# A fused attention and mixture-of-experts kernel: the start and the first score items of its projection stage rearranged

## The reference

```python
x = x + _L0_attn_a_ref(_layernorm(x), Wq, Wk, Wv, Wo)      # this layer's projection is what changes
x = x + _L0_ffn_ref(_layernorm(x), ...)
x = x + _L0_attn_b_ref(_layernorm(x), ...)
x = x + _L0_ffn_ref(_layernorm(x), ...)

def _L0_attn_a_ref(x, Wq, Wk, Wv, Wo):
    q = (x @ Wq.T).reshape(Bx, Tx, H, dk)
    k = (x @ Wk.T).reshape(Bx, Tx, H, dk)
    v = (x @ Wv.T).reshape(Bx, Tx, H, dk)
    scores = jnp.einsum('bthd,bshd->bhts', q, k) / math.sqrt(dk)
    scores = jnp.where(causal_mask, -jnp.inf, scores)
    attn = jax.nn.softmax(scores, axis=-1)
    ...
```

## Time and profile before

| | us |
|---|---|
| median of 3 runs | 1771.57 |
| lowest and highest of them | 1766.8, 1778.27 |
| the profiled execution, whole | 1780.99 |
| its span (first to last instruction in the profile) | 1779.3 |
| TensorE busy in the span | 1642.0 |
| VectorE busy in the span | 1278.2 |
| projection stage, up to the last item's matmuls | 131.5 |

### The profile page before, as it was taken

How to read it: one execution, slowest core, us unless ns; L and a number is a source line. 1 busy time by engine, 2 the same in 40 slices (tenths; PEclk the granted TensorE clock), 3 DMA queues, 4 the chain that set the end, 5 groups by cost and what they waited for, 6 DMA issues and landing times. The chain is left out here.

```text
span 1779.3 us, 35884 instructions
## 1 busy us (share of the span) xinstructions
PE 1642.0 (92%) x11140; PEld 1206.5 (68%) x11141; DVE 1278.2 (72%) x2670; ACT 1048.0 (59%) x1851; POOL 796.1 (45%) x773
## 2 busy tenths in 40 slices
PE   7889999999999794999999998699975999999998
PEld 3454444444443683999999998344544999999997
DVE  5678788888882667677777776358886777777776
ACT  3336677776777443666666664546654666666664
POOL 5431112112121122666666665225542566666664
PEclk9999999999999875999999999899975999999999
DMA  4655254453531752332232222301112222222222
GB/s 138 188 142 130 86 135 111 114 131 103 121 96 49 159 184 70 86 47 48 48 49 48 48 49 36 109 1 48 48 47 82 45 47 47 47 47 47 47 47 38
DMA packets 102667, 140.85 MB, mean 79 GB/s; under 512 B 18160, under 2 KB 86768, under 8 KB 99504
## 3 DMA queue, kind: packets, MB, share of 16 engines
q1 hardware_dynamic: 65638, 90.88, 19.5%
q0 software_dynamic: 31808, 37.32, 13.0%
q10 hardware_dynamic: 5130, 11.54, 1.9%
HBM read 74.21 MB, written 56.69 MB: 74 GB/s over the span
## 5 line engine op out<-in xcount | busy, mean ns | idle before, releaser
L555 ACT ACTIVATE a_Pt<-a_p_st 128x512 f32<-128x512 f32 (+2 forms) x624 | 302.2, 592 | 132.2 <-PE a_p_st L636 131.8
L582 DVE TENSOR_REDUCE mx<-a_p_sn 128x2 f32<-128x256 f32 (+1 forms) x600 | 333.3, 627 | 63.1 <-PE a_p_sn L619 53.7
L1321 ACT COPY R<-values_then_w 128x1024 f32 x284 | 283.0, 1044 | 38.7 <-issue 21.4
L1270 PE MATMUL e_p_g<-e_tT,R 128*128 128x128 f32 x2272 | 280.5, 277 | 1.5 <-ACT e_tT L1313 1.5
L1270 PE MATMUL e_p_l<-e_tT,R 128*128 128x128 f32 x2272 | 277.8, 276 | 0.0
L1282 PE MATMUL e_p_y<-w,e_hid 128*128 x1136 | 269.6, 380 | 5.8 <-DVE e_hid L1390 5.8
L1270 PEld LDWEIGHTS e_p_g<-e_tT,R 128*128 128x128 f32 x2272 | 268.3, 194 | 2.4 <-ACT e_tT L1313 2.3
L1270 PEld LDWEIGHTS e_p_l<-e_tT,R 128*128 128x128 f32 x2272 | 266.3, 193 | 0.1
L532 POOL TENSOR_SCALAR_AFFINE_SELECT a_Pt<-a_Pt 128x512 f32<-128x512 f32 x128 | 81.5, 637 | 363.5 <-ACT a_Pt L555 363.5
L1282 PEld LDWEIGHTS e_p_y<-w,e_hid 128*128 128x128 f32 x1136 | 205.3, 191 | 28.2 <-issue 6.2
L619 PE MATMUL a_p_sn<-Kst,Qst 96*128 96x128 bf16 (+1 forms) x720 | 219.7, 332 | 1.9 <-PEq L151 1.5
(11 more groups left out here) (213 smaller groups left out, 2396.8 us busy)
## 6 DMA issues: line engine op xcount, KB each, us to landing
qk_parts<-a_part SPq DMA_DIRECT2D x64, 192.0 KB, 3.2
a_Vst<-values_then_w SPq DMA_DIRECT2D x16, 512.0 KB, 18.2
o_rows<-a_OT ACTq DMA_DIRECT2D x32, 256.0 KB, 2.8
values_then_w<-in_mlp SPq DMA_DIRECT2D x16, 512.0 KB, 4.6
t_rows<-R SPq DMA_DIRECT2D x16, 512.0 KB, 3.0
Kst<-qk_parts SPq DMA_DIRECT2D x14, 384.0 KB
Qst<-qk_parts SPq DMA_DIRECT2D x14, 384.0 KB
X<-in_x SPq DMA_DIRECT2D x8, 512.0 KB, 6.1
```

Of the source, the lines that this page charges most:

```text
L555: act.activation(weights(kb, slice(h, h + n), a, b), p_st[:, i % RING, 0:n * (b - a)].rearrange("p (n w) -> p n w", n=n), ACT.Exp, scale=D ...
L582: dve.tensor_reduce(mx[:, hs[0]:hs[-1] + 1, place], p_sn[:, (s + k) % RING, 0:w * len(hs)].rearrange("p (h w) -> p h w", w=w), AX.X, ALU.m ...
L1270: mm = pe.matmul(bank[:, s, c * P:(c + 1) * P], copied[:, s, k, at:at + P], tT[:, s, k * P:(k + 1) * P], start=(k == 0), stop=(k == KD - 1))
L1321: act.copy(copied[:, s, :, cols], g["w1"][:, bass.ds(e, 1), :, cols].rearrange("p a k n -> p (a k) n")).then_inc(copied_done, 1)
```

## The change

Four things, all in `project_qkv`.

1. The first chunk is loaded in two halves of 256 KB, half 0 by SyncE, half 1 by ScalarE's queue, both as their first DMA. SyncE waits for half 1 before it loads chunk 1. VectorE takes statistics and moments of half 0, then of half 1, then inverts and normalises half 0, then half 1, with semaphores of its own for half 0. ScalarE takes two square roots of two columns instead of one of four. TensorE transposes each half as it is ready, and waits for the weights only behind the transposes.
2. ScalarE runs a Sqrt on the eps constant into a small tile `trial` as soon as eps is there, so the table load stands in front of that one.
3. TensorE begins with WARM = 14 bf16 matmuls of the identity against itself, 512 columns each, into p_first, whose result nobody reads. `identb`'s completion now counts in `ident_done` for them.
4. The pads of V are written in four quarters by GpSimd, one at the end of each of chunks 4 to 7. The table `shares` moves the first items: none in slots 0 to 4 of chunk 4, five in its slot 5, and one more in slot 5 of chunks 5 and 6. Chunk 7 has the same items as before.

```diff
@@ -108,6 +108,9 @@
+WARM = 14
+
+
 def project_qkv(nc, mem, g, x_dram, qk_dram):
@@ -132,6 +135,9 @@
     pad_done = mem.sem("pad_d")
+    x_front, st_front, mv_front, std_front, rstd_front, n_front, tried = (
+        mem.sem(s) for s in ("x_f", "st_f", "mv_f", "std_f", "rstd_f", "n_f", "tried"))
+    trial = mem.sb("trial", [P, 1])
     part_out = g["part_out"]
@@ -139,7 +145,7 @@
-        shares = {4: (0, 0, 0, 2, 3, 2), 5: (2, 2, 2, 2, 2, 1), 6: (2, 2, 2, 2, 2, 1), 7: (2, 2, 2, 2, 2, 1)}
+        shares = {4: (0, 0, 0, 0, 0, 5), 5: (2, 2, 2, 2, 2, 2), 6: (2, 2, 2, 2, 2, 2), 7: (2, 2, 2, 2, 2, 1)}
         order = [(k, i) for k in shares for i in range(6) for _ in range(shares[k][i])]
@@ -147,6 +153,10 @@
         return g["V"][:, bass.ds(2 * (c - s), HG), kb:kb + 2, :, 0:DK]
+
+    def load_half(eng, half, landed):
+        eng.dma_start(g["X"][:, 2 * half:2 * half + 2, :],
+                      x_dram[2 * half * P:2 * (half + 1) * P, :].rearrange("(t p) d -> p t d", p=P)).then_inc(landed, 16)
@@ -172,19 +182,22 @@
-            load(0, 0)
+            load_half(sp, 0, x_front)
             for m, w in enumerate((g["WqT"], g["WkT"], g["WvT"])):
                 sp.dma_start(w3[:, m], w.rearrange("(k p) n -> p k n", p=P)).then_inc(w_in, 16)
+            sp.wait_ge(x_in[0], 16)
             load(1, 1)
...
             first_constants(pool, g)
-            pads = g["V"][:, :, :, :, :].rearrange("p u k h c -> p (u k h) c")
-            pool.memset(pads[:, :, DK:PAD], 0.0).then_inc(pad_done, 1)
-            pool.wait_ge(pad_done, 1)
-            pool.memset(pads[:, :, DK:DK + 1], 1.0)
+
+            def pads(i):
+                at = g["V"][:, 4 * i:4 * (i + 1), :, :, :].rearrange("p u k h c -> p (u k h) c")
+                pool.memset(at[:, :, DK:PAD], 0.0).then_inc(pad_done, 1)
+                pool.wait_ge(pad_done, i + 1)
+                pool.memset(at[:, :, DK:DK + 1], 1.0)
@@ -196,6 +209,8 @@
                     pool.wait_ge(g["ones_done"], c)
+                if c >= 4:
+                    pads(c - 4)
             paired(pool, CH, step, CH // 2 - 1)
@@ -219,8 +234,13 @@
+            load_half(act, 1, x_in[0])
             act.wait_ge(g["eps_done"], 1)
-            root(0, 0)
+            act.activation(trial[:, :], g["eps"][:, :], ACT.Sqrt).then_inc(tried, 1)
+            act.wait_ge(mv_front, 1)
+            act.activation(std[:, 0, 0:2], mv[:, 0, 0:2, 1], ACT.Sqrt, bias=g["eps"][:, :]).then_inc(std_front, 1)
+            act.wait_ge(mv_done, 1)
+            act.activation(std[:, 0, 2:4], mv[:, 0, 2:4, 1], ACT.Sqrt, bias=g["eps"][:, :]).then_inc(std_done, 1)
             turned(0, 0)
@@ -274,12 +294,26 @@
-            dve.wait_ge(x_in[0], 16)
-            statistics(0, 0)
-            dve.wait_ge(stats_done, 1)
-            moments(0, 0)
-            inverse(0, 0)
-            normalise(0, 0)
+            front = ((x_front, st_front, mv_front, std_front, rstd_front, n_front),
+                     (x_in[0], stats_done, mv_done, std_done, rstd_done, n_done))
+            for half, (landed, counted, known, rooted, inverted, ready) in enumerate(front):
+                dve.wait_ge(landed, 16)
+                for t in (2 * half, 2 * half + 1):
+                    last = dve.bn_stats(stats[:, t, :], g["X"][:, t, :])
+                last.then_inc(counted, 1)
+                dve.wait_ge(counted, 1)
+                for t in (2 * half, 2 * half + 1):
+                    last = dve.bn_aggr(mv[:, 0, t, :], stats[:, t, :])
+                last.then_inc(known, 1)
+            for half, (landed, counted, known, rooted, inverted, ready) in enumerate(front):
+                two = slice(2 * half, 2 * half + 2)
+                dve.wait_ge(rooted, 1)
+                dve.reciprocal(rstd[:, 0, two], std[:, 0, two]).then_inc(inverted, 1)
+                dve.wait_ge(inverted, 1)
+                for t in (2 * half, 2 * half + 1):
+                    last = dve.tensor_scalar(n[:, 0, t, :], g["X"][:, t, :], mv[:, 0, t, 0:1],
+                                             rstd[:, 0, t:t + 1], ALU.subtract, ALU.mult)
+                last.then_inc(ready, 1)
@@ -321,9 +355,6 @@
         def _(pe):
-            pe.wait_ge(w_in, 48)
-            pe.wait_ge(g["ident_done"], 1)
-
             def turn(c, s):
@@ -331,7 +362,17 @@
-            turn(0, 0)
+            pe.wait_ge(g["ident_done"], 2)
+            for _ in range(WARM):
+                pe.matmul(p_first[:, 0, :], g["identb"][:, :], g["identb"][:, :].unsqueeze(1).to_broadcast([P, 4, P]),
+                          start=True, stop=True, skip_group_check=True)
+            for half, ready in enumerate((n_front, n_done)):
+                pe.wait_ge(ready, 1)
+                for k in range(KD):
+                    for t in (2 * half, 2 * half + 1):
+                        mm = pe.transpose(p_t[:, k, t * P:(t + 1) * P], n[:, 0, t, k * P:(k + 1) * P], g["ident"][:, :])
+            mm.then_inc(t_done, 1)
+            pe.wait_ge(w_in, 48)
@@ -2040,7 +2081,7 @@
     pool.affine_select(out=g["identb"][:, :], in_=g["identb"][:, :], compare_op=ALU.not_equal, fill=1.0, base=0,
-                       pattern=[[-1, P]], channel_multiplier=1)
+                       pattern=[[-1, P]], channel_multiplier=1).then_inc(g["ident_done"], 1)
     pool.affine_select(out=g["maskb"][:, :], in_=g["maskb"][:, :], compare_op=ALU.is_ge, fill=NEG, base=0,
```

## The result

The changed kernel takes 1759.1 us (median of 6 runs, 1752.95 to 1772.88), the kernel before 1771.43 (6 runs). The ratio is 0.9944, with a 95% interval of 0.9918 to 0.9971: 9.9 us less (5.1 to 14.5), where 9.4 was forecast. The medians themselves lie 12.3 us apart. A second set of runs of the same two kernels gave 0.9925 (0.9886 to 0.9964). The profiled execution took 1772.88 us, its span is 1771.1, against 1780.99 and 1779.3: 8.1 us less.

What follows compares the result with a forecast made beforehand. TensorE was taken as the bound, working 11.73 us of a 12.21 us step. Start 3.3, clock 2.5, items 3.6 and pads 0 sum to 9.4 us: 1771.6 to 1762.2, with 1754 to 1771 holding 8 in 10.

Steps and rivals of the forecast that it cites:

- The start: Before chunk 0's products: they begin at about 10.6 and not 13.92, 3.3 us gained, ends 2.8 and 4.3.
- The pads: GpSimd's quarter fills at the end of chunks 4 to 7: cost 0, or 1.2 if pieces take twice as long.
- The clock: TensorE in chunk 0: the 14 added matmuls may bring full clock, between 0 and 2.54 us, 2.5 taken.
- Rival A: TensorE's clock falls again before chunk 0's products, so chunk 0 keeps its 2.5 us: 1764.7; chance 0.25.
- Chunk 4: Moved first items end TensorE's wait for Qst and the slow clock: gain 4.4 us, ends 3.0 and 5.0.
- the prediction's own sign: In the changed kernel's timeline, a chunk 4 over 17 us would prove a step wrong; 15.1 was expected.
- Chunks 5 and 6: One item more in each, behind the second half of the values: 0.4 us each, 0.8 in all, ends 0.4 and 1.6.
- rival B: Items' gain given back in chunks 5 and 6 as VectorE becomes the bound, or Qst lands late: 1764 to 1767; chance 0.13.
- The barrier: Behind chunk 7: GpSimd's pads end at 131.8, VectorE's last reduction at 132.59, so cost 0 with 0.8 us of cover.
- Rival C: Later stages: the shifted start loses more of TensorE's clock, making the kernel slower, 1773 to 1776 with some more; chance 0.12.

Runs made afterwards that it cites:

- rows early: Changed kernel with the rows of chunk 5 loaded one step earlier, chunks 4 and 5 issued together in step 2; ratio to before 0.9926.
- second profile: Profile of the changed kernel run again with no edit; second stage starts at 122.25, ratio to before 0.9925.
- before with new shares: Kernel of before with only the new table of item shares; ratio to before 0.9958.
- whole first chunk: Changed kernel with the first chunk loaded and processed whole, the other edits kept; one run, products of chunk 0 start at 10.43, second stage at 124.88.
- late pads: Kernel of before with only the pads in quarters at the end of chunks 4 to 7; ratio to before 0.9992.
- pads first: Changed kernel with the four quarters of the pads written one behind the other at the start; ratio to before 0.9939.

## Why the prediction was right, and where not

- **The start, 3.3 us forecast.** It was 4.0 in the first profile and 4.4 in the second, just over the upper bound of 4.3. Half 0 landed at 4.41 (4.6 taken), and the wait for the root went (0.5 to 0.9 of it due to the trial). The term that was missized is the normalisation: 1.22 a half taken, 0.73 measured. The overlap of the first four transposes with the second normalisation, which the sum counted on, did not happen in the first profile: the 14 matmuls ended at 8.18, so the eight transposes began at 8.02. In the profile where they ended first, at 7.25 (rows early), four transposes ran from 7.19 and the products began at 9.52, 0.37 us earlier. Fewer of these matmuls were not tried.
- **The pads, cost 0 and 0.1 us given back at the start.** This is the step that failed: written in quarters at the start, they cost 3.8 us of the start and 1.8 of chunk 0 (the two long fills of before were not tried there). I read the 2.44 us of the earlier trace rows as the price of normalising four tiles, though GpSimd's fills stood beside it; without them it is 1.38. The row that I held against the skill's rule was a copy of values, and that copy reads PSUM; it says nothing of an operation that reads and writes SBUF. By the Trainium skill (SBUF — State Buffer, Who interferes with whom) VectorE in a mode that uses the shared port pair and GpSimd shut each other out for a whole instruction, and tensor_scalar, which the normalisation is, is among the operations that can enter such a mode. The trace agrees, with 4.16 us against 0.73, though no run shows which mode the normalisation was in. I also looked for its harm in chunks 4 to 7, where the fills went, and not at the start, where they came from. The fills at the end of chunks did no harm: chunks 5 and 6 kept their 16.6 and 16.3, and a copy of values at 74.64 took its 0.69 us in the middle of a fill of 1.80.
- **The clock, 2.5 us.** Right: 2.56 against the profile of before. Five other profiles without a raised clock show chunk 0 at 13.91 to 14.23, so 1.7 to 2.0 is the usual gain, and 2.5 was the high end. Rival A, that gaps bring the clock down before the products, did not come about: it stayed up over the gap of 0.83 us in front of the products. In a gap of 2.97 us it did fall.
- **Chunk 4, 4.4 us.** The forecast of 15.1 is what the second profile shows (15.14, with 0.78 us of the new wait in it; without any it is 14.66), and the first is far off (18.17). The mechanism was right, as the two kernels with the rows early show (5.6 us between the tables); what was missing is the next wait. By the prediction's own sign, a chunk 4 over 17 us, the first profile proves a step wrong. I checked when chunk 1's rows land, and not chunk 5's, though the 0.62 us that VectorE waited for them before was in the trace: this transfer had no reserve. It was asked for no later in the step, but took 12.7 and 15.0 us instead of 11.2, and VectorE waited 0.8 and 3.1 us.
- **Chunks 5 and 6, 0.4 each.** 0.14 and 0.00. The extra item stands where TensorE needs no read for it, as rival B's counter-argument said; the charge was too high in these profiles. In two others with the new table (before with new shares, whole first chunk) chunk 6 took 16.68, 0.38 more, and that isn't explained.
- **The barrier, 0.** 0.38 us, cause open.

The sum for the first profile: 4.0 + 2.6 + 1.35 − 0.1 − 0.4 = 7.4 us, which is 132.99 less 125.57. For the second, 10.7. The whole time, 9.9 us with an interval of 5 to 14.5, can't choose between them. A start taken too small, a wait forgotten and items overcharged cancelled in part, and that is luck.

Rival C of the prediction, a different clock in later stages, needs a word. From the second stage's first matmul to the end of the span it is 1646.3 us in the profile of before and 1645.5 in the changed kernel's, but 1631.7 to 1637.5 in eleven others and 1644.5 in the kernel with late pads, whose granted clock means 0.942; the two long ones have 0.944 and 0.945, the others 0.950 to 0.955. So 12 us of difference come and go behind the stage with no relation to the edits. Nothing suggests that the change moved them.

## What to carry to other kernels

A duration in a trace is the price beside its neighbours: before one is used for a forecast, look at what the other engines did in it, GpSimd's fills beside VectorE above all. For every transfer that a step asks for, not only the first, compare how long before its use it is issued with how long it takes, and with how much that time varies: one that was just in time (0.62 us late before) can be the next wait. And an edit that seems to be housekeeping, like where constants are written, can be what the others rest on: judge edits together and by leaving each out.

## What the runs showed that I had not expected

- Fills on GpSimd hold up a float32 tensor_scalar of VectorE from SBUF to SBUF: two tiles take 0.73 us alone and 4.16 while fills followed one another, each ending 0.14 us behind a fill. GpSimd's subtraction goes with the same: in the steps of chunks 0 to 4 four tiles take 2.21 us, not 1.38, and nearly all of the excess is in one tile, the fourth, which runs from 18.11 for 1.25 us instead of 0.41 and ends at 19.36, 0.15 us behind the subtraction begun at 17.96 (below, from the changed kernel). In the next two steps the first tile is the one beside a subtraction, and the four take 1.89 and 2.02. What it would bring to move it was not tried.

```profile
17.15 2.21 DVE L285 TENSOR_SCALAR a_n<-X,a_mv,a_rstd 128x256 f32<-128x256 f32 x4
...
17.96 1.25 POOL L206 TENSOR_TENSOR a_part<-a_rest,a_part 128x512 bf16<-128x512 f32 x1 [0.77 <-ACT a_part L254]
```

- TensorE's clock, once raised, stayed at 2.4 GHz through a stretch in which TensorE did eight transposes and then nothing for 0.83 us (chunk 0 takes 12.19 or 12.20 us in eight profiles), and fell to 1.2 within a gap of 2.97 us without work (pads first). In chunk 4 of the first profile it fell 1.1 us behind a gap of 2.56.
- In the first profile of the changed kernel a 512 KB load of rows lands 3.8 to 4.8 us after its issue in the steps up to chunk 2, and 15.0 and 14.0 us after it in chunks 3 and 4, where the loads of Kst and Qst run too; the issue alone then took 1.85 and 4.92 us instead of 0.60.
